# A convolution and a routed FFN in one program: the use of a batch's rows and tables moved by a few steps, and three of the products added on VectorE

## What is computed

```python
xn = _ln_c(x)                                   # normalised over channels
h = einsum('bchw,oc->bohw', xn, reduce_w) + reduce_b          # 32 channels
kern = einsum('bchw,oc->bohw', h, span_w) + span_b            # 49 taps x 16 groups
x = x + (kern.reshape(b, G, 1, 49, H, W) * patches(xn)).sum(axis=3)
t = to_tokens(x)                                # 12544 tokens of 128
flat = _ln_t(t)
probs = softmax(flat @ router_w.T); gates = top2(probs) / sum
t = t + sum_e gates[e] * ((silu(flat @ w1[e].T) * (flat @ w3[e].T)) @ w2[e].T)   # 8 experts, hidden 341
```

## Time and profile before

| | us |
|---|---|
| median of 3 runs (1734.08 to 1741.15) | 1740.23 |
| the profiled execution | 1734.33 |
| its span, first to last instruction | 1732.5 |
| step 225 (tile 9, unit 0) begins at | 389.0 |
| the convolution ends at about | 1460 |

### The profile page before, as it was taken

How to read it: one execution, slowest core, us unless ns; L and a number is a source line. 1 busy time by engine, 2 the same in 40 slices (tenths; PEclk the granted TensorE clock), 3 DMA queues, 4 the chain that set the end, 5 groups by cost and what they waited for, 6 DMA issues and landing times.

```text
span 1732.5 us, 23003 instructions
## 1 busy us (share of the span) xinstructions
PE 1288.3 (74%) x7827; PEld 1054.8 (61%) x7827; DVE 1138.5 (66%) x2163; ACT 399.8 (23%) x866; POOL 1280.7 (74%) x977
## 2 busy tenths in 40 slices
PE   1888687869669688587885896948949668778773
PEld 0766466657557576476774675837737557556552
DVE  3899898887767586576765877658747767422220
ACT  2111111122122322122312222222212113433331
POOL 3777977878958969489686796886958858765555
PEclk9999998989889899699897998979979889889996
DMA  3111111122233322222322223222231123675652
GB/s 107 36 46 48 51 47 48 51 77 46 34 91 67 77 46 33 77 68 43 89 35 72 68 37 100 40 70 57 46 76 41 29 85 65 150 186 140 138 132 27
DMA packets 93343, 120.39 MB, mean 69 GB/s; under 512 B 11531, under 2 KB 72428, under 8 KB 93082
## 3 DMA queue, kind: packets, MB, share of 16 engines
q1 hardware_dynamic: 53802, 90.97, 17.2%
q0 software_dynamic: 39424, 27.96, 11.6%
HBM read 78.92 MB, written 42.65 MB: 70 GB/s over the span
## 4 chain that ended last, share of the span: by engine, by line
POOL 48%; PE 15%; issue 13%; DVE 11%; DMA 8%; ACT 2%; SPq 1%; POOLq 0%; DVEq 0%; ACTq 0%
POOL acc_p L943 18%; POOL out L964 15%; POOL xs L952 8%; PE acc_ps L536 5%; DVE prod L712 5%; DMA out<-y_tok,idx 4%; PE kern_ps L521 4%; POOL rstd_ln L927 3%; POOL acc_p L939 2%; DMA xb<-xs 2%; DMA xs<-rows_x,slots 2%; PE bank L503 1%; PE bank L509 1%; PE h_ps L554 1%; PE h_ps L555 1%
## 5 line engine op out<-in xcount | busy, mean ns | idle before, releaser
L712 DVE TENSOR_TENSOR prod<-kern_ps,xn 128x896 f32<-128x896 f32 x672 | 705.4, 1081 | 179.3 <-PE kern_ps L521 167.7
L943 POOL TENSOR_TENSOR acc_p<-acc_p,prod 128x896 f32<-128x896 f32 x252 | 551.7, 2189 | 26.2 <-DVE prod L712 19.3
L521 PE MATMUL kern_ps<-h_stack,span 98*128 98x448 f32 x1372 | 450.9, 425 | 121.2 <-DVE prod L712 117.9
L964 POOL DMA_INDIRECT out<-y_tok,idx x224 | 350.7, 1566 | 128.7 <-DVE idx L883 50.9
L536 PE MATMUL acc_ps<-ident_sb,prod 128*112 128x128 f32 x3024 | 417.8, 285 | 4.3 <-DVE x L890 4.3
L536 PEld LDWEIGHTS acc_ps<-ident_sb,prod 128*112 128x112 f32 x3024 | 370.8, 140 | 44.8 <-DVE x L890 11.9
L521 PEld LDWEIGHTS kern_ps<-h_stack,span 98*128 98x128 f32 x1372 | 236.9, 202 | 220.9 <-DVE prod L712 186.5
L952 POOL DMA_INDIRECT xs<-rows_x,slots x224 | 219.2, 979 | 152.3 <-DVE slots L797 105.5
L554 PE MATMUL h_ps<-xf_hi,wb 128*114 128x512 f32 x336 | 158.3, 471 | 40.9 <-DVE hid L852 27.1
L852 DVE TENSOR_TENSOR hid<-silu,h_ps 114x512 f32<-114x512 f32 x168 | 114.7, 683 | 102.8 <-PE h_ps L558 81.8
L509 PEld LDWEIGHTS bank<-w2b,hid 114*128 114x128 f32 x1344 | 161.3, 196 | 29.9 <-DVE h_stack L876 18.2
(11 more groups left out here) (103 smaller groups left out, 1025.4 us busy)
## 6 DMA issues: line engine op xcount, KB each, us to landing
wb<-wexp SPq DMA_DIRECT2D x56, 684.0 KB, 4.5
xb<-xs SPq DMA_DIRECT2D x56, 264.0 KB, 4.1
w2b<-in_w SPq DMA_DIRECT2D x56, 171.0 KB
xt<-in_x SPq DMA_DIRECT2D x28, 224.0 KB, 3.6
out<-x SPq DMA_DIRECT2D x28, 224.0 KB, 2.7
wexp<-wb SPq DMA_DIRECT2D x8, 684.0 KB
xs<-rows_x,slots POOLq DMA_INDIRECT x224, 2.4
out<-y_tok,idx POOLq DMA_INDIRECT x224
```

The costliest lines, as they stand in the source:

```text
L521: last = mm(kern_ps[:, g % 2, i, 0:N], span[:, k * C:(k + 1) * C], h_stack[:, t % 2, :], start=True, stop=True)
L712: v.tensor_tensor(pair_rows(dst), kern_ps[:, g % 2, :, 0:N].rearrange("p i (r w) -> p i r w", w=W), window(start + PAIRS[u][0], PAIRS[u][1 ...
L943: g_.tensor_tensor(acc_p[:], acc_p[:], prod[:, (t * TAPS + u) % PRING, :], ALU.add).then_inc(s_padd, 1)
L964: g_.indirect_dma_start(out=out, out_offset=bass.IndirectOffsetOnAxis(ap=idx[:, b % XBRING, q:q + 1], axis=0), in_=y_tok[:, b % 2, q * C:( ...
```

## The change

There are three parts. **Later use**: a batch is ready two steps later (`LANDING` 5 in place of 3); the transposes "mx" of its first blocks may come 3 steps behind `READY` in place of 1, and the first slot 5 in place of 2; rows of other blocks are loaded 8 steps ahead of their transposes in place of 4. So between a group's last scatter and the first transposes there are 8 steps in place of 4. **Tables later, and fewer**: `table` runs three steps behind `place` (before the product of unit 3 of the tile, and not before that of unit 0), and only for the eleven groups in `TABLES`; groups 4 and 6 have no batch of their own, their blocks go with the next. The sizes of the batches of groups 2 to 8 were 3, 4, 3, 4, 3, 4, 3 and are 3, 4, 0, 7, 0, 7, 3. **Adds on DVE**: from tile 9 on DVE adds product 3 to 5, 11 to 13 and 19 to 21 (SBUF to SBUF, 128 x 896), right behind the product of unit 6, 14 and 22, and PE transposes only the sums: eleven products in place of fourteen. That is 19 tiles x 3 = 57 adds, and 24 transposes fewer a tile.

```diff
+BY_VECTOR = ((3, 5), (11, 13), (19, 21))
+VECTOR_FROM = 9
...
+TABLES = (2, 3, 5, 7, 8, 9, 10, 11, 12, 13, 14)
+for _g in range(NG):
+    if _g not in TABLES:
+        FULL[_g] = FULL[_g - 1] if _g else 0
...
+LANDING = 5
...
-    READY.append(_S + 3)
+    READY.append(_S + LANDING)
...
-    _S = max(_S, READY[BATCH_OF[_b]] + 2)
+    _S = max(_S, READY[BATCH_OF[_b]] + 5)
...
-    _S = max(_ready + 1, SLOT_AT[(_b - 2) * SLOTS + 5] if _b >= 2 else 0)
+    _S = max(_ready + 3, SLOT_AT[(_b - 2) * SLOTS + 5] if _b >= 2 else 0)
...
-    LOAD_AT.setdefault(max(_ready - 2, _x[_b][0] - 4), []).append(("x", _b))
+    LOAD_AT.setdefault(max(_ready - 2, _x[_b][0] - 8), []).append(("x", _b))
...
+def pairs_of(t):
+    return BY_VECTOR if t >= VECTOR_FROM else ()
...
-    _left = list(BY_PE)
+    _merged = {a: b for a, b in pairs_of(_t)}
+    _left = [u for u in BY_PE if u not in _merged]
...
-            if _left and at(_t, _left[0]) + 2 <= _S:
+            if _left and at(_t, _left[0]) + (4 if _left[0] in _merged.values() else 2) <= _S:
...
-                if S == ROUTER_AT[NG - 1] + J_R2 + 1:
+                if S == ROUTER_AT[NG - 1] + J_RANK + 5:
                     pad()
...
                     if name == "rank":
                         place(t)
-                        if BATCH[t]:
-                            table(t)
-                        else:
-                            v.memset(nothing[:], 0.0).then_inc(s_tab, 1)
...
+                for g in range(NG):
+                    if BATCH[g] and S == ROUTER_AT[g] + J_RANK + 4:
+                        table(g)
...
                 if 0 <= p < TILES:
                     unit(p, j)
+                    for k, (first, second) in enumerate(pairs_of(p)):
+                        if j == second + 1:
+                            g = p * TAPS
+                            a, b = prod[:, (g + first) % PRING, :], prod[:, (g + second) % PRING, :]
+                            dve.wait_ge(s_prod, g + second + 1)
+                            v.tensor_tensor(b, a, b, ALU.add).then_inc(s_vadd, 1)
```

More of the change, by code:

```diff
@@ L43 @@
 ADDS = len(BY_POOL) - 1
-SUMS = len(BY_PE) + 1
 PRING = 8
+BY_VECTOR = ((3, 5), (11, 13), (19, 21))
+VECTOR_FROM = 9
 GROUPS_OF = [(2 * i, 2 * i + 1) for i in range(13)] + [(26,), (27,)]
@@ L305, in build @@
         s_x1 = sem("s_x1")
+        s_vadd = sem("s_vadd")
         s_spill = [sem(f"s_spill{i}") for i in range(3)]
@@ L367, in consumer @@
                 eng.wait_ge(s_padd, t * ADDS + max(BY_POOL.index(u), 1))
+            elif u in [a for a, _ in pairs_of(t)]:
+                eng.wait_ge(s_vadd, (t - VECTOR_FROM) * len(BY_VECTOR) + [a for a, _ in pairs_of(t)].index(u) + 1)
             else:
@@ L404, in pad @@
             def pad():
-                sp.wait_ge(s_tab, NG)
+                sp.wait_ge(s_tab, len(TABLES))
                 for e in range(EXPERTS):
@@ L416, in load_block @@
                     if b == BLOCK0[g]:
-                        sp.wait_ge(s_tab, g + 1)
+                        sp.wait_ge(s_tab, TABLES.index(g) + 1)
                         last = GROUPS_OF[g][-1]
@@ L528, in sum_unit @@
                     pe.wait_ge(s_prod, t * TAPS + u + 1)
+                    for k, (_, second) in enumerate(pairs_of(t)):
+                        if u == second:
+                            pe.wait_ge(s_vadd, (t - VECTOR_FROM) * len(BY_VECTOR) + k + 1)
                     src = prod[:, (t * TAPS + u) % PRING, :]
```

## The result

The changed kernel takes **1765.81 us** (median of 4, 1764.33 to 1766.92), the kernel before 1739.83 beside it (4 runs, 1734.08 to 1741.15). The ratio is **1.0155 [1.0131, 1.018]**: 26 us slower, with an interval clear of 1. The prediction, 1698 us with a range of 1650 to 1735, was wrong in sign.

What follows compares the result with a forecast made beforehand. No engine full; POOL, nearest to full, bounds the kernel, with stalls for `xb` and `slots` once in each even tile. 1734.3 - 83.0 + 14 + 38 - 5 = 1698 us, range 1650 to 1735.

Steps and rivals of the forecast that it cites:

- use and tables (-83.0 + 14 - 5): POOL's `slots` waits go, -83.0; two `xf_lo` ahead of unit 0 in 7 batches, +14; tile 8's shorter stall, -5.
- later sums, less the saved transposes: PE in tiles 9 to 27: 24 transposes fewer a tile, 63 us of PE, costed at nothing; later sums not priced.
- The 100 us on DVE I cost at nothing on the path.: 57 adds of 1.75 us on DVE, covered by 208 us of its idle time in tiles 9 to 27: 0.
- The 83.0 us on POOL go: POOL's nine waits for `slots` in tiles 9 to 27 vanish, since `slots` come before POOL is free: -83.0 us.
- two of the nine: Of nine batches with stalls in tiles 9 to 27, two go with the tables of groups 4 and 6.
- The late table, 0 (or -2.6 a batch): `table` behind unit 2: no cost, its reading load some 40 steps away; 2.6 us leaves each batch's tile start.
- The adds on POOL, +38: Each of 57 DVE adds delays POOL 0.66 us when it comes between two POOL adds: +38, bounds 0 and +62.
- The add's duration, 1.75 us, minimum 1.09: Each new DVE add with two SBUF inputs takes 1.09 us plus a wait, about 1.75 us in the mean.
- +62 on POOL: By the skill's port rule alone, DVE adds come first each time, costing POOL 1.09 us each: +62 instead of +38.
- Rival D: DVE becomes the limit, all 100 us of adds on the path, POOL's delay hidden: 1760 us, slower; chance 0.11.
- Rivals B and C: B: `xb` stall returns, 1733 us, chance 0.13. C: POOL's tile-start waits go too, 1640 or 1626, chance 0.10.
- The tail, 272 forecast: The rest behind the convolution, limited by POOL's issue of 96 `add_rows`, is unchanged at 272 us, 6 either side.

Runs made afterwards that it cites:

- e1: The changed kernel without the adds on DVE, PE transposing fourteen products in all tiles; later use and fewer, later tables stay: 1691.76 us.
- e4: The changed kernel with the 57 DVE add instructions left out, products 3, 11 and 19 missing from the sum, PE's later sums kept: 1723.07 us.
- e7: The changed kernel with each add taking one input from PSUM, ahead of the product, so sums are other numbers: 1755.20 us.
- e9: As e5, but PE's sum of product 21 alone stands four steps behind its product, those of 5 and 13 two: 1718.72 us.
- e5: As e4, but PE's sums of products 5, 13 and 21 stand two steps behind the product and not four: 1687.48 us.
- e3: As e1, but with a table and a batch of its own for groups 4 and 6 again: 1735.95 us.
- e11: As e6, plus the later first transposes (3 steps behind READY) and first slot (5 steps) alone: 1682.05 us.
- e6: The kernel before with the tables of groups 4 and 6 skipped and nothing else: 1681.63 us.
- e10: As e6, plus the table three products later, with the padding of the last group three steps later: 1694.44 us.
- e8: As e1, but with tables only for groups 3, 5, 7, 9 and 11 to 14: 1689.10 us.
- e12: As e1, but with the earlier landing, use and load steps of the kernel before for groups 13 and 14: 1697.93 us.

## Why the prediction was wrong

The prediction's sum, beside what the runs give for its terms:

| term | forecast | measured | from |
|---|---|---|---|
| start | 1734.3 | 1739.2 | the profiled execution; the median of before beside e1 |
| use and tables (-83.0 + 14 - 5) | -74 | -47 | e1 - before |
| the add instructions (POOL +38, DVE 0) | +38 | +43 | after - e4 |
| later sums, less the saved transposes | 0 | +31 | e4 - e1 |
| sum | 1698 | 1766 | |

Three steps failed: the sums of PE that stand later, the credit for the wait taken away, and the DVE time "at nothing on the path", which the sum hides because POOL's term was too large by about as much.

**"The 100 us on DVE I cost at nothing on the path."** The cover named was DVE's idle time, 208 us of it in the stretch. What the runs showed in its place: e4 gives 43 us for the adds, 0.75 us for each of 1.72, so more than half of their time found cover and the rest did not. The adds stand in the line of products, `kern_ps` is a ring of two, and an add between two products makes PE wait for the next place (PE behind DVE: 68.9 us before, 138.4 in e4, 194.0 after). Where the cover lies can be read off the starts of DVE's products in e4 and in the changed kernel, as the time from product j to the next, added over the 19 tiles. With the add behind product 6 this step grows from 36.0 to 72.0 us, behind product 22 from 48.8 to 71.1. Behind product 14 it grows from 23.0 to 49.1, but there the step ahead of it shrinks from 88.2 to 57.9: in e4 DVE waits for PE in front of product 14 (42 us in all, 30 with the add), so of the three only this add lies where there was time. Idle time summed over a stretch is no cover for an instruction at a fixed place. Of the 74 us of the part (after - e1):

- 11 are what goes away when one input of the add is in PSUM (after - e7), the lock between DVE and GpSimd with the reserve made there;
- 32 are the rest of the adds' price (e7 - e4), the time of an add in the line, 0.56 us for each;
- 31 are the sum of unit 21, two steps later, at the tile's end (e9 - e5), and 4 the other two late sums (e4 - e9; 2 by the ratios, within the intervals);
- about -4 are 24 transposes a tile fewer (e5 - e1, by medians; these two ran on different chips, and their ratios to before, 0.9706 and 0.9721, say -3).

The items add to 74 by construction, since each is the difference of two neighbours in the chain after, e7, e4, e9, e5, e1; in another order the single prices could be others.

**Missed altogether: the late sums, put at nothing.** `(4 if ... else 2)` stands in the diff, and the prediction counted the transposes that go ("I cost it at nothing too: PE is not the limit"), not the step at which those that remain stand. They cost 36 us (e4 - e5), 31 of them by the sum of 21. It had named the place ("POOL's first add of a tile waits for the product of unit 2 and for PE's last sum") and looked there only for what DVE puts in front of unit 0.

**The removed wait, -83.0 + 14 - 5: too much by 27 us, and the part of the change wrong.** It was forecast at 74 us and gave 47.4 (e1). "The 83.0 us on POOL go" failed: without any adds POOL still waits 36.4 us in 8 waits for `slots` (e1), where under 15 was forecast. The forecast also put the gain to the later use. e3 gives 3 us for the later use together with the later `table`, with all tables, and e11 gives 0 for the later transposes and slots with eleven; e6 gives 57.5 for the tables alone, against the "two of the nine" of the prediction, which by its own 83 / 9 would be 18. Two errors: two more stalls go than batches, and a stall is worth more than POOL's part of it (57.5 us of time against 37.1 us less wait on POOL and 77.2 less on PE). And what is taken from PE's wait by moving the work behind it is in good part waited for again at `base`, `rows_x` and `kern_ps` (e3), or at the end (e11). Taking a stall away and moving it are two edits.

**The late table, 0 (or -2.6 a batch): wrong.** It costs 13 us (e10). The check was that no reader is late; what stands behind it on DVE, the product of unit 3 and those that PE and POOL want next, was not priced.

So from 1739.8: -57.5 tables skipped, +13 table late, and -3 for landing, use and loads together give e1's 1692; +74 adds gives 1766. The -3 is the remainder, not a run of its own.

**The adds on POOL, +38: near as busy time, too large as a term of the path.** POOL is busy 28 us more than before, 27 more than without the adds (e4: 825.9), 0.47 us each and not 0.66. But e7, which takes these 27 us away, is only 10.6 us faster. The prediction's lower bound, nothing "if it falls into a DMA issue of POOL", is refuted: DMA issues bear 21 of the 27. That +38 and 0 together come near the 43 us measured is luck: the path has more of DVE in it and less of POOL.

**The add's duration, 1.75 us, minimum 1.09:** 1.72 and 1.07, right (the prediction's own terms, 1.09 + 0.72, make 1.81). That an instruction with one input in PSUM isn't stretched is shown by e7. The Trainium skill says so ("SBUF — State Buffer", section "Who interferes with whom": at most one SBUF input, no contention with GpSimd), and this case's runs agree, 1091 ns in the median against 1232 and a mean of 1718. The sum that the prediction made from the same section, +62 on POOL, is farther from the 27 measured than +38 was.

**Rival D** was the nearest, 1760 with a chance of 0.11, but its number is in part luck: it has 100 us of adds on the path and 74 us of gain, where 74 and 47 were measured. Its threshold, slower from 1.3 us exposed for each add, rests on that gain; with 47 us it is 0.83. Its mechanism was half right: POOL waits for products in the middle of a tile only 20 times, 29.5 us (30.7 in e1, without adds), and DVE is busy 77% (842.7 of 1096.5), not over 90%. DVE is no limit by its load. It stands in a cycle with PE, in which each waits some 193 us for the other. Such a cycle is no mark of the adds: e4 has it without them, with 212.2 us of DVE's waits and 138.4 of PE's. What the adds do is to shift it to PE's side. Rivals B and C found no support: the wait for `xb` didn't come back, and POOL waits more at a tile's start (69.9 us, 57.9 before).

**The tail, 272 forecast, 283.7 measured.** It is 275.9 to 287.6 in the versions with the later use (e8 aside), 279.3 in e10, which has only the later `table` and padding, and 272.6 in e6, with 95 to 96 `add_rows` left in all these. So the late table has a part of it, in the one profiled run of each. e12 excludes the later landing, use and loads of groups 13 and 14. What makes the rest stays open.

## What to carry to other kernels

Price an instruction at its place in the line: name the wait that ends last right there, and take as its cover only idle time that lies between it and the next instruction that someone waits for. In this loop with two places of `kern_ps`, DVE was 69% busy before in the stretch (743.7 of 1071), and still 43 of 98 us of new work came on the path. When an edit shortens work but makes its input come later, look up at which step the rest of that work now stands, and what is released by its end; here that cost some 35 us, where the shorter work gave 4. Two errors can cancel in a sum, so compare term by term and not the total. And a stall that comes once in each batch was removed by fewer batches, and gave three quarters of the wait that went, until the work left behind the convolution grew (e8), while a later use mostly moved it: e6, the kernel before with two tables left out, takes 1681.63 us, 0.967 [0.964, 0.970], and nothing added to it made it faster.

## What was not expected of the hardware

- An addition on DVE with two SBUF inputs makes the *issue* of an indirect DMA on POOL longer: scatter issues 968 ns in the mean without such adds beside them (e4, e7), 1055 with 57 of them in the stretch; accumulating ones 1578 and 1646.
- The add itself has a long tail: 1232 ns in the median, 4029 at most. The POOL adds of the same stretch (L969) hardly change, 2294 ns in the mean against 2277 in e4 and e7.
- The same transposes took twice the time in one place as in another a few us later. In e9, behind steps in which PE waited for `base` and `xf_lo`, the clock granted from 493.8 to 497.5 is 0.50, that is 1.2 GHz, and from 497.9 on 1.00:

```profile
493.80:497.50 3.70, 3.70 (x18) 3.68 (x17) 1.76 (x3) 1.39 (x2) 0.00 (x0) 0.50 0.00 0
497.90:499.40 1.50, 1.50 (x14) 1.49 (x13) 1.30 (x3) 0.00 (x0) 0.00 (x0) 1.00 0.00 0
```

  The 16 transposes of 493.82 took 0.23 us each, the 8 of 500.72 0.13. e5 has the same clock at this place behind the same waits, and its 8 transposes of 490.57 took 0.24 us each:

```profile
490.50:494.40 3.90, 3.90 (x17) 3.50 (x16) 2.90 (x5) 1.44 (x2) 0.00 (x0) 0.50 0.00 0
```

  So the late sum of e9 did not lower the clock; 12 transposes stand in the slow stretch in e5 and 16 in e9. In the stage as a whole the clock explains little: e5 was granted 0.87 and is as fast as e1 with 0.89.
